# Graph-attention network on one core: the load phase's constants, centring, conversions and clearing in another order

## The chip, the cores and the metric

The kernel runs on one core of one Trainium2 chip. The metric is device time in microseconds (us) of that core. A core has five engines that work beside each other and meet by semaphores: TensorE (PE, matrix products, its weight loads shown as PEld), VectorE (DVE), ScalarE (ACT), GpSimd (POOL) and SyncE (SP), which here only issues transfers. Each engine runs its own list of instructions in the order written. Every engine's wait (`wait_ge`) holds back all that is queued behind it on that engine.

## The reference

Four graph layers run over one graph of 2048 nodes with 64 features. The adjacency matrix is a 2048 x 2048 int32 array. Every layer is preceded by a layer norm and a ReLU, and its result is added to x:

```
h = relu(layernorm(x)); x = x + gat(h, adj, W0, a0)
h = relu(layernorm(x)); x = x + gat(h, adj, W1, a1)
h = relu(layernorm(x)); x = x + two_step_gat_with_mlp(h, adj, ...)
h = relu(layernorm(x)); x = x + key_query_attention_with_powers(h, adj, ...)

gat(h, adj, W, a): Wh = h @ W
  e = leaky_relu((Wh @ a_src)[:, None] + (Wh @ a_dst)[None, :])
  att = softmax(where(adj > 0, e, -9e15), axis=1)
  return elu(att @ Wh)
```

The kernel counts four such attention passes (two of them inside the third layer) and the last one with keys and queries.

## The kernel before

**Tiling.** Nodes are split in 16 blocks of 128 (`NB`) and, the other way, in two column halves of 1024 (`NCH`). x lies transposed, 64 features times two strips on the 128 partitions, 512 columns for each column half. The adjacency comes as 32 blocks of 128 x 1024 int32 (512 KB each): blocks 0 to 15 are those of the first column half, 16 to 31 those of the second. They are staged in nine slots; a slot is loaded again when its block is converted. A block is converted twice: VectorE turns it into a bf16 mask in `nadj` (L1411), and an fp8 copy in `adj` is made by VectorE (L1418) for every third of the first 16 blocks, by ScalarE (L485) for the others.

**Constants.** One array `cst` of 128 x 1600 fp32 (800 KB) holds the identity (`ident`), the centring matrix (`center`), the columns that sum a strip (`half`), the weights `wt` with their transposes `wTt`, the attention vectors `av`, `lwT`, `atv`, `lbv`, and others. ScalarE issues its transfer (L406); SyncE issues x (L342) and then the blocks (L350). A second array `late` comes at the end of the list.

**Load phase, in the order of each engine.** TensorE waits for the constants, computes attention vectors of the third layer's passes (L611, L613) into the bank `M`, waits for VectorE to copy them (L1400, L1401), multiplies all attention vectors with the weights (L618), waits for VectorE to write these into the weight tile (L1404), and only then waits for x and centres it (`centre`, L631) into a PSUM bank of each column half. ScalarE squares the two centred halves (L411), VectorE clips them (L1138), TensorE sums the squares (`variances`, L651), VectorE writes the variances (L1143) and GpSimd takes their inverse roots (L372). TensorE then computes the norm of the weights (L861) and the features of both halves (`features`, L670), VectorE scales them by the roots (L1164, L1175), splits the row vector in three bf16 parts (L1185, L1130 to L1134), and TensorE and ScalarE spread it over the partitions (L678, L415, L685, L421). VectorE's list mixes `convert(n)` for the first nine blocks into this.

**First layer.** With the levels (L1201, L1204) TensorE takes a maximum over neighbours block by block (`chunk_levels`, L745), which needs the fp8 copies of blocks 0 to 15; the codes (L1258), products (L756), shifts (L427) and targets (L1270, L1274) follow. Then all four passes run over 16 blocks and two halves: VectorE writes the scores to PSUM (L1282), TensorE adds the mask (L763), ScalarE takes the exponential (L439), TensorE multiplies with the features (L771) and sums the rows (L791). In the first pass VectorE's list holds the conversions of the last blocks between the scores. The order of all lists is written out by hand.

**Clearing.** GpSimd clears small constants and `Kst` (L365) before the semaphore `consts` that all engines wait for; VectorE clears `Qst` (L1407) in the load phase. Both tiles are first written by `keys_split`, in the last layer.

Of the kernel before, what the change touches and what calls it, by code (L numbers as in the profile page):

```python
# [6 lines left out]
P = 128  # L7
N = 2048
F = 64
NB = N // P  # L10
CH = 1024
NCH = N // CH
# [4 lines left out]
GAT = 4  # L17
# [17 lines left out]
_at = 0  # L35
for _name, _width in (("ident", P), ("center", P), ("pick", 2), ("wt", GAT * 2 * (F + 2)),
                      ("half", 2), ("win", WIN), ("wTt", GAT * P), ("av", GAT * 2), ("lwT", 2 * P), ("atv", 2),
                      ("lbv", 2)):
    CONST[_name] = (_at, _width)
    _at += _width  # L40
WIDTH = _at
LATE = {"mw": (0, 3 * P), "wkq": (3 * P, 4 * EMB), "mb": (3 * P + 4 * EMB, 1),
        "restore": (3 * P + 4 * EMB + 1, P)}
# [3 lines left out]
def program(nc, xT_d, cst_d, late_d, adjT_d, out_d):  # L47
# [4 lines left out]
    with ctx:  # L52
# [6 lines left out]
        def sem(name):  # L59
            return ctx.enter_context(nc.semaphore(name))  # L60
# [110 lines left out]
        ld_x = sem("ld_x")  # L171
        ld_c = sem("ld_c")
        ld_late = sem("ld_late")
        ld_adj = [sem(f"ld_adj{k}") for k in range(SLOTS)]
# [100 lines left out]
        block = ctx.enter_context(nc.Block())  # L275
        N_C = 7

# [53 lines left out]
        def feat(hh):  # L331
            return slice(F * hh, F * (hh + 1))
# [7 lines left out]
        @block.sync  # L340
        def _(sp):
            sp.dma_start(x[:], xT_d.rearrange("c p n -> p c n")).then_inc(ld_x, 16)  # L342
            for n in range(NCH * NB):
                held = [m for m in range(n) if SLOT_OF[m] == SLOT_OF[n]]
                if held:
                    sp.wait_ge(adj_ready, held[-1] + 1)
                    if by_dve(held[-1]):
                        sp.wait_ge(adj8_dve, copies_by_dve(held[-1]))
                b = n % NB
                sp.dma_start(slot(n), adjT_d[b * P:(b + 1) * P, cols(n // NB)]).then_inc(ld_adj[SLOT_OF[n]], 16)  # L350
            sp.dma_start(late[:], late_d).then_inc(ld_late, 16)
            for c in range(NCH):
                sp.wait_ge(out_ready, c + 1)
                sp.dma_start(out_d[c], x[:, c, :]).then_inc(st_out, 16)
            sp.wait_ge(st_out, 16 * NCH)

        @block.gpsimd
        def _(pool):
# [5 lines left out]
            pool.memset(lnS[:], math.log(1 - SLOPE)).then_inc(consts, 1)  # L364
            pool.memset(Kst[:], 0.0).then_inc(consts, 1)  # L365
            pool.wait_ge(consts, N_C)
            n_root = [0]

# [36 lines left out]
        def _(act):  # L405
            act.dma_start(cst[:], cst_d).then_inc(ld_c, 16)  # L406
            act.wait_ge(consts, N_C)

            def square(n):
# [196 lines left out]
        def _(pe):  # L606
            pe.wait_ge(consts, N_C)
            pe.wait_ge(ld_c, 16)
            for l in range(2):
                for t in range(2):  # L610
                    pe.matmul(M[0:F, 2 * l + t:2 * l + t + 1], lwT[:, l, t * F:(t + 1) * F],  # L611
                              atv[:, l:l + 1], start=True, stop=True)
                last = pe.matmul(M[:, 8 + l:9 + l], lbv[:, l:l + 1].broadcast_to([32, P]), atv[:, l:l + 1],  # L613
                                 start=True, stop=True)
            last.then_inc(pe_prep, 1)
            pe.wait_ge(prep_ready, 1)
            for l in range(GAT):
                last = pe.matmul(M[:, 16 + 2 * l:18 + 2 * l], wTt[:, l, :], av[:, l, :], start=True, stop=True)  # L618
            last.then_inc(pe_prep, 1)
            pe.wait_ge(prep_ready, 3)  # L620
            pe.wait_ge(dve_const, 2)

            def repeat(bank_of, count):
# [223 lines left out]
            def key_rows(c):  # L847
# [4 lines left out]
                last.then_inc(kT_psum, 1)  # L852

            for n in range(NCH):
                if n == 0:
                    pe.wait_ge(ld_x, 16)
                centre(n)
            for n in range(NCH):
                variances(n)
            pe.wait_ge(wsq_ready, 1)  # L860
# [253 lines left out]
        def _(dve):  # L1114
# [254 lines left out]
            def keys_split(c):  # L1369

                link(dve.tensor_copy(parts[:, :, :, 0, :], kq[:]))
                link(dve.tensor_tensor(kqr[:], kq[:], parts[:, :, :, 0, :], ALU.subtract))
# [26 lines left out]
            dve.wait_ge(pe_prep, 1)  # L1399
            dve.tensor_copy(cb[:], M[:, 8:10])  # L1400
            dve.tensor_copy(av[:, 2:4, :], M[0:F, 0:4].rearrange("p (l t) -> p l t", l=2)).then_inc(prep_ready, 1)  # L1401
            dve.wait_ge(pe_prep, 2)
            for hh in range(2):
                dve.tensor_copy(wt4[feat(hh), :, hh, F:F + 2],  # L1404
                                M[feat(hh), 16:16 + 2 * GAT].rearrange("p (l t) -> p l t", l=GAT)).then_inc(prep_ready, 1)
            weight_squares()
            dve.memset(Qst[:], 0.0).then_inc(dve_const, 1)  # L1407

# [11 lines left out]

            convert(0)
            convert(1)
            for n in range(NCH):
                clip(n)
            for n in range(NCH):
                variance(n)
            convert(2)
            convert(3)
            weight_norms()
# [273 lines left out]
```

## Time and profile before

| what | value |
|---|---|
| three runs | 599.19, 594.17, 599.13 us; median 599.13 us |
| profiled execution's own time | 598.86 us |
| its span, first to last instruction | 597.1 us |
| mean granted TensorE clock | 0.974 |
| PE busy | 527.5 us, 88% |
| DVE busy | 393.9 us, 66% |
| ACT busy | 290.1 us, 49% |
| POOL busy | 30.8 us, 5% |
| HBM read | 18.40 MB |

Busy time is a share of the whole span. Matrix products are pipelined and their ends modelled, so a busy TensorE isn't one at its peak. The span is less than the execution's time by what lies around it. The granted clock is the share of 2.4 GHz that the chip lets TensorE have.

### The profile page before, as it was taken

Reading aid. Unit: us, or ns where it says so; the run is one execution under the profiler, and the core shown is the slowest. Engines: PE = TensorE matmul, PEld = TensorE weight load, DVE = VectorE, ACT = ScalarE, POOL = GpSimd, SP = SyncE. Lnnn points to the kernel's source line nnn. Section 1 sums busy time; section 2 is a strip of 40 time slices with the busy share of each in tenths; the row PEclk is TensorE's granted clock in tenths of the full one; section 3 lists DMA queues with packets and bytes.
Section 4 is the critical chain, followed back from the end, with each engine's and each line's share of the span. In section 5 each row is a group of like instructions: output and inputs, shape, how many; then the busy total and the mean of one; then the engine's idle time right before and its main releaser. Section 6 shows DMA issues by size and latency. Waiting matters only on the chain.

```text
span 597.1 us, 7591 instructions
## 1 busy us (share of the span) xinstructions
PE 527.5 (88%) x3136; PEld 198.5 (33%) x3136; DVE 393.9 (66%) x545; ACT 290.1 (49%) x314; POOL 30.8 (5%) x29
## 2 busy tenths in 40 slices
PE   4578997998998998998988998999868789999997
PEld 3422223343223343323243223344332234433332
DVE  2888779548989448989637989544999985110000
ACT  0487964524665525665524665446858685000000
POOL 1500000211000110000100000023000000000000
PEclk9788999999999999999989999999999899999999
DMA  8968100000000000000000000000000000000000
GB/s 323 343 235 290 45 1 0 1 2 1 0 1 1 2 0 2 1 1 0 1 1 1 1 2 1 0 1 2 0 0 1 0 2 0 1 2 0 1 8 28
DMA packets 5490, 19.40 MB, mean 32 GB/s; under 512 B 592, under 2 KB 592, under 8 KB 5456
## 3 DMA queue, kind: packets, MB, share of 16 engines
q1 hardware_dynamic: 5312, 18.11, 8.3%
q10 hardware_dynamic: 144, 0.82, 0.3%
q8 instruction: 24, 0.39, 0.3%
q14 instruction: 10, 0.08, 0.0%
HBM read 18.40 MB, written 0.52 MB: 32 GB/s over the span
## 4 chain that ended last, share of the span: by engine, by line
PE 57%; DVE 26%; ACT 7%; issue 7%; DMA 1%; POOL 1%; POOLq 0%; DVEq 0%; ACTq 0%
PE PROD L771 11%; PE X L1001 9%; DVE X L1282 9%; PE X L763 7%; PE PROD L1001 7%; PE S L791 6%; DVE aB L1550 6%; ACT big L439 4%; DVE big L1294 2%; DVE nadj L1567 2%; ACT big L485 1%; PE M L626 1%; DMA cst<-in_cst 1%; PE M L725 1%; DVE big L1291 1%
## 5 line engine op out<-in xcount | busy, mean ns | idle before, releaser
L439 ACT ACTIVATE big<-X,v 128x1024 f32<-128x1024 f32 x128 | 141.6, 1113 | 103.8 <-PE X L763 103.1
L1282 DVE SCALAR_TENSOR_TENSOR X<-wB,v,aB 128x1024 f32<-128x1024 f32 x128 | 163.4, 1294 | 27.7 <-ACT big L439 26.3
L771 PE MATMUL PROD<-big,Wh 128*64 128x512 f32 x512 | 135.7, 611 | 1.5 <-ACT big L439 1.3
L763 PE MATMUL X<-nadj,bigI 128*64 128x512 bf16 x512 | 77.9, 384 | 22.4 <-DVE X L1282 22.0
L763 PEld LDWEIGHTS X<-nadj,bigI 128*64 128x64 bf16 x512 | 25.5, 109 | 105.6 <-DVE X L1282 73.5
L791 PE MATMUL S<-big,onesf 128*32 128x512 f32 x400 | 53.3, 604 | 2.4 <-DVE big L1294 2.4
L771 PEld LDWEIGHTS PROD<-big,Wh 128*64 128x64 f32 x512 | 31.4, 136 | 51.9 <-issue 29.1
L1001 PE MATMUL PROD<-big,Wh 128*64 128x512 f32 x128 | 32.8, 634 | 9.7 <-ACT big L554 9.7
L372 POOL TENSOR_TENSOR rr<-var,mhalf 128x8 f32<-128x8 f32 x8 | 15.0, 1877 | 305.2 <-DVE var L1143 305.2
L1001 PE MATMUL PROD<-nadj,Wh 128*64 128x512 f32 x128 | 29.1, 598 | 0.4 <-ACT nadj L554 0.4
L1001 PE MATMUL X<-big,Wh 128*64 128x512 f32 x128 | 28.6, 595 | 0.0
L1001 PE MATMUL X<-nadj,Wh 128*64 128x512 f32 x128 | 28.0, 593 | 0.0
L485 ACT ACTIVATE big<-nadj 128x1024 fp8e4<-128x1024 bf16 x26 | 25.8, 1054 | 1.4 <-DVE nadj L1411 1.4
L1294 DVE TENSOR_TENSOR big<-big 128x1024 f32<-128x1024 f32 x21 | 25.6, 1219 | 0.4
L427 ACT ACTIVATE aB<-X,nvb,nvs 128x512 f32<-128x512 f32 x14 | 9.8, 775 | 25.5 <-PE X L756 25.5
L974 PE MATMUL X<-nadj,bigI 128*128 128x512 bf16 x64 | 19.3, 382 | 2.5 <-ACT big L544 1.4
L554 ACT ACTIVATE big<-big 128x1024 f32<-128x1024 f32 x16 | 16.8, 1057 | 8.8 <-DVE big L1567 8.8
L1567 DVE TENSOR_TENSOR nadj<-nadj,aB 128x1024 f32<-128x1024 f32 x16 | 18.4, 1218 | 3.0 <-ACT aB L550 2.9
L1567 DVE TENSOR_TENSOR big<-big,aB 128x1024 f32<-128x1024 f32 x16 | 19.4, 1224 | 0.5
L1411 DVE TENSOR_SCALAR nadj<-big 128x1024 bf16<-128x1024 int32 x28 | 18.9, 692 | 0.5 <-DMA big<-in_adjT 0.5
L977 PE MATMUL X<-wB 96*128 96x512 bf16 x64 | 19.1, 379 | 0.0
L1550 DVE TENSOR_TENSOR aB<-aB,big 128x1024 f32<-128x1024 f32 x15 | 18.4, 1224 | 0.4
(293 smaller groups left out, 574.7 us busy)
## 6 DMA issues: line engine op xcount, KB each, us to landing
big<-in_adjT SPq DMA_DIRECT2D x28, 512.0 KB, 6.9
aB<-in_adjT SPq DMA_DIRECT2D x4, 512.0 KB, 7.8
cst<-in_cst ACTq DMA_DIRECT2D x1, 800.0 KB, 5.8
x<-in_xT SPq DMA_DIRECT2D x1, 512.0 KB, 6.1
out<-x SPq DMA_DIRECT2D x2, 256.0 KB, 2.0
late<-in_late SPq DMA_DIRECT2D x1, 272.5 KB, 5.5
```

The lines of the kernel that those rows point to most:

```text
L439: act.activation(prob[:, t % U, :], X[t % 2][:], ACT.Exp, bias=v2[l % 2][:, k:k + 1]).then_inc(p_ready, 1)
L485: act.activation(adj[:, b, part], nadj[:, b, part], ACT.Identity, bias=1.0, saturate=False).then_inc(adj8_act, 1)
L763: last = pe.matmul(X[t % 2][feat(side), hh * BANK:(hh + 1) * BANK], bigI[:, feat(side)], nadj[:, k, half_cols(c, hh)], start=False, stop=T ...
L771: last = pe.matmul(PROD[c][feat(hh), :], Wh[l % 2][:, k, :], prob[:, t % U, hh * BANK:(hh + 1) * BANK], start=k == 0, stop=k == NB - 1)
L791: last = pe.matmul(S[32 * strip:32 * strip + 32, :], onesf[:, 0:32], src[:, hh * BANK:(hh + 1) * BANK], start=k == first_sum(c_all), stop= ...
L974: pe.matmul(X[s % 2][:, hh * BANK:(hh + 1) * BANK], bigI[:], nadj[:, jb, half_cols(c, hh)], start=True, stop=False)
L977: last = pe.matmul(X[s % 2][:, hh * BANK:(hh + 1) * BANK], KQ[0:KPAD, jb // CB, 1, (jb % CB) * P:(jb % CB + 1) * P], KQ[0:KPAD, c, 0, hh * ...
L1001: last = pe.matmul(out[feat(hh), :], src[:, jb, :], kept(c, jb)[:, hh * BANK:(hh + 1) * BANK], start=jb == 0, stop=jb == NB - 1)
L1282: dve.scalar_tensor_tensor(X[t % 2][:], wB[:, cols(c)], v8[l % 2][:, k:k + 1], aB[:, cols(c)], ALU.max, ALU.add).then_inc(x_written, 1)
L1294: ins = dve.tensor_tensor(acc[c], acc[c], prob[:, t % U, :], ALU.add)
L1550: ins = dve.tensor_tensor(accf[:, cols(c)], accf[:, cols(c)], kept(c, k), ALU.max)
L1567: dve.tensor_tensor(kept(c, k), kept(c, k), accf[:, cols(c)], ALU.add).then_inc(s_lowered, 1)
```

## The change

The constants are put in another order, so that `ident`, `center`, `half`, `lwT`, `atv`, `lbv` and `av` are its first 526 columns. SyncE loads these 526 columns first, then x, then block 0, then the other 1074 columns (`pick`, `wt`, `win`, `wTt`) with a semaphore of their own (`ld_w`), then the blocks from 1 on. TensorE centres x behind the first small products, and L618 moves between the variances of the two halves. The small products go to a corner of the bank `X[0]` instead of `M`. VectorE's list takes the first conversions apart. ScalarE gets one dummy activation ahead of everything. GpSimd clears both `Kst` and `Qst`, behind the semaphore `consts`, and `keys_split` waits for that.

```
-for _name, _width in (("ident", P), ("center", P), ("pick", 2), ("wt", GAT * 2 * (F + 2)),
-                      ("half", 2), ("win", WIN), ("wTt", GAT * P), ("av", GAT * 2), ("lwT", 2 * P), ("atv", 2),
-                      ("lbv", 2)):
+for _name, _width in (("ident", P), ("center", P), ("half", 2), ("lwT", 2 * P), ("atv", 2), ("lbv", 2),
+                      ("av", GAT * 2), ("pick", 2), ("wt", GAT * 2 * (F + 2)), ("win", WIN), ("wTt", GAT * P)):
+FIRST = CONST["pick"][0]
...
-        N_C = 7
+        N_C = 6
...
         def _(sp):
+            sp.dma_start(cst[:, 0:FIRST], cst_d[:, 0:FIRST]).then_inc(ld_c, 16)
             sp.dma_start(x[:], xT_d.rearrange("c p n -> p c n")).then_inc(ld_x, 16)
             for n in range(NCH * NB):
+                if n == 1:
+                    sp.dma_start(cst[:, FIRST:WIDTH], cst_d[:, FIRST:WIDTH]).then_inc(ld_w, 16)
...
-            pool.memset(Kst[:], 0.0).then_inc(consts, 1)
             pool.wait_ge(consts, N_C)
+            pool.memset(Kst[:], 0.0).then_inc(keys_clear, 1)
+            pool.memset(Qst[:], 0.0).then_inc(keys_clear, 1)
...
         def _(act):
-            act.dma_start(cst[:], cst_d).then_inc(ld_c, 16)
             act.wait_ge(consts, N_C)
+            act.activation(seed[:, 0:1], lnS[:], ACT.Square)
...
             pe.wait_ge(ld_c, 16)
             (the first small products: M becomes X[0])
             last.then_inc(pe_prep, 1)
-            pe.wait_ge(prep_ready, 1)
-            for l in range(GAT):
-                last = pe.matmul(M[:, 16 + 2 * l:18 + 2 * l], wTt[:, l, :], av[:, l, :], start=True, stop=True)
-            last.then_inc(pe_prep, 1)
-            pe.wait_ge(prep_ready, 3)
-            pe.wait_ge(dve_const, 2)
...
+            pe.wait_ge(ld_x, 16)
             for n in range(NCH):
-                if n == 0:
-                    pe.wait_ge(ld_x, 16)
                 centre(n)
-            for n in range(NCH):
-                variances(n)
+            variances(0)
+            pe.wait_ge(ld_w, 16)
+            pe.wait_ge(prep_ready, 1)
+            for l in range(GAT):
+                last = pe.matmul(X[0][:, 16 + 2 * l:18 + 2 * l], wTt[:, l, :], av[:, l, :], start=True, stop=True)
+            last.then_inc(pe_prep, 1)
+            variances(1)
+            pe.wait_ge(prep_ready, 3)
+            pe.wait_ge(dve_const, 2)
             pe.wait_ge(wsq_ready, 1)
...
             def keys_split(c):
+                dve.wait_ge(keys_clear, 2)
...
             dve.wait_ge(pe_prep, 1)
             (the copies to cb and av[:, 2:4]: M becomes X[0])
-            dve.wait_ge(pe_prep, 2)
-            for hh in range(2):
-                dve.tensor_copy(wt4[feat(hh), :, hh, F:F + 2],
-                                M[feat(hh), 16:16 + 2 * GAT].rearrange("p (l t) -> p l t", l=GAT)).then_inc(prep_ready, 1)
-            weight_squares()
-            dve.memset(Qst[:], 0.0).then_inc(dve_const, 1)
...
             convert(0)
+            clip(0)
             convert(1)
-            for n in range(NCH):
-                clip(n)
-            for n in range(NCH):
-                variance(n)
+            variance(0)
+            clip(1)
             convert(2)
+            dve.wait_ge(ld_w, 16)
+            dve.wait_ge(pe_prep, 2)
+            for hh in range(2):
+                dve.tensor_copy(wt4[feat(hh), :, hh, F:F + 2],
+                                X[0][feat(hh), 16:16 + 2 * GAT].rearrange("p (l t) -> p l t", l=GAT)).then_inc(prep_ready, 1)
+            weight_squares()
+            variance(1)
             convert(3)
             weight_norms()
```

## Rows read from the trace of the kernel before

**Rows 1.** The page: the span, and the transfer of the result to memory

```profile
span 597.1 us, 7591 instructions
...
out<-x SPq DMA_DIRECT2D x2, 256.0 KB, 2.0
```

**Rows 2.** The chain that ended last, from the start: start us, us, what

```profile
0.72 5.82 DMA cst<-in_cst
...
8.25 0.53 PE M L613 x2
9.07 1.88 PE M L618 x8
...
13.55 1.28 ACT L411
...
44.80 1.29 DVE X L1282
```

**Rows 3.** TensorE in order of time: start us, us, engine, line, tiles, shapes, count

```profile
11.39 3.48 PE L631 MATMUL PROD<-x,cst 128*128 128x512 f32 x4 [0.45 <-DVE cst L1404]
15.49 1.05 PE L651 MATMUL M<-cst,sq 128*128 128x2 f32 x8 [0.62 <-ACT sq L411]
16.41 1.03 PE L651 MATMUL S<-cst,sq 128*128 128x2 f32 x8
...
17.68 1.12 PE L670 MATMUL M<-cst,g 128*128 128x132 f32 x4
...
48.41 3.46 PE L771 MATMUL PROD<-big,Wh 128*64 128x512 f32 x8
...
54.64 1.94 PE L771 MATMUL PROD<-big,Wh 128*64 128x512 f32 x8
...
109.28 1.12 PE L635 MATMUL PROD<-x,cst 128*128 128x512 f32 x2
```

**Rows 4.** VectorE in order of time, 10 to 20 us

```profile
10.97 0.36 DVE L1404 COPY cst<-M 64x8 f32<-64x8 f32 x2 [1.96 <-PE M L618]
...
11.86 0.62 DVE L1411 TENSOR_SCALAR nadj<-big 128x1024 bf16<-128x1024 int32 x1
...
19.71 0.17 DVE L1164 TENSOR_TENSOR uv<-M,rr 128x8 f32<-128x8 f32 x1 [0.19 <-PE PROD L670]
```

**Rows 5.** Transfers issued in 0 to 12 us: count, KB, median us to landing

```profile
big<-in_adjT SPq DMA_DIRECT2D x8, 512.0 KB, 9.8
cst<-in_cst ACTq DMA_DIRECT2D x1, 800.0 KB, 5.8
x<-in_xT SPq DMA_DIRECT2D x1, 512.0 KB, 6.1
aB<-in_adjT SPq DMA_DIRECT2D x1, 512.0 KB, 13.2
```

**Rows 6.** Stretches: busy time by engine, granted clock, DMA share, GB/s

```profile
0.00:3.00 3.00, 0.00 (x0) 0.00 (x0) 0.00 (x0) 0.00 (x0) 1.50 (x11) 1.00 0.29 57
3.00:6.50 3.50, 0.00 (x0) 0.00 (x0) 0.00 (x0) 0.00 (x0) 0.00 (x0) 1.00 1.00 402
6.50:8.00 1.50, 1.33 (x9) 1.33 (x10) 0.36 (x2) 0.00 (x0) 0.00 (x0) 1.00 0.93 249
8.00:20.00 12.00, 10.61 (x46) 8.09 (x46) 6.68 (x19) 4.37 (x5) 2.76 (x2) 0.91 1.02 413
32.00:36.00 4.00, 3.89 (x22) 1.17 (x18) 4.00 (x8) 4.00 (x6) 0.00 (x0) 0.64 0.11 44
```

**Rows 7.** SyncE's issues in order of time: the first eight blocks

```profile
1.21 4.59 SPq L350 DMA_DIRECT2D big<-in_adjT  x8
```

**Rows 8.** GpSimd in order of time: the roots of the variances

```profile
17.24 3.71 POOL L372 TENSOR_TENSOR rr<-var,mhalf 128x8 f32<-128x8 f32 x2 [15.21 <-DVE var L1143]
```

**Rows 9.** Stretches, for TensorE's granted clock (the column before DMA share)

```profile
17.50:21.00 3.50, 3.50 (x17) 3.48 (x18) 3.24 (x10) 1.06 (x1) 3.50 (x3) 0.55 1.03 411
48.00:52.00 4.00, 4.00 (x14) 1.15 (x16) 4.00 (x5) 3.02 (x4) 0.00 (x0) 0.57 0.66 230
52.00:60.00 8.00, 8.00 (x58) 2.56 (x56) 6.18 (x9) 6.96 (x7) 0.00 (x0) 1.00 0.88 306
```

More of the change, by code:

```diff
@@ L172, in program @@
         ld_c = sem("ld_c")
+        ld_w = sem("ld_w")
+        keys_clear = sem("keys_clear")
         ld_late = sem("ld_late")
@@ L610, in _ @@
                 for t in range(2):
-                    pe.matmul(M[0:F, 2 * l + t:2 * l + t + 1], lwT[:, l, t * F:(t + 1) * F],
+                    pe.matmul(X[0][0:F, 2 * l + t:2 * l + t + 1], lwT[:, l, t * F:(t + 1) * F],
                               atv[:, l:l + 1], start=True, stop=True)
-                last = pe.matmul(M[:, 8 + l:9 + l], lbv[:, l:l + 1].broadcast_to([32, P]), atv[:, l:l + 1],
+                last = pe.matmul(X[0][:, 8 + l:9 + l], lbv[:, l:l + 1].broadcast_to([32, P]), atv[:, l:l + 1],
                                  start=True, stop=True)
             last.then_inc(pe_prep, 1)
-            pe.wait_ge(prep_ready, 1)
-            for l in range(GAT):
-                last = pe.matmul(M[:, 16 + 2 * l:18 + 2 * l], wTt[:, l, :], av[:, l, :], start=True, stop=True)
-            last.then_inc(pe_prep, 1)
-            pe.wait_ge(prep_ready, 3)
-            pe.wait_ge(dve_const, 2)
             def repeat(bank_of, count):
@@ L1399, in _ @@
             dve.wait_ge(pe_prep, 1)
-            dve.tensor_copy(cb[:], M[:, 8:10])
-            dve.tensor_copy(av[:, 2:4, :], M[0:F, 0:4].rearrange("p (l t) -> p l t", l=2)).then_inc(prep_ready, 1)
-            dve.wait_ge(pe_prep, 2)
-            for hh in range(2):
-                dve.tensor_copy(wt4[feat(hh), :, hh, F:F + 2],
-                                M[feat(hh), 16:16 + 2 * GAT].rearrange("p (l t) -> p l t", l=GAT)).then_inc(prep_ready, 1)
-            weight_squares()
-            dve.memset(Qst[:], 0.0).then_inc(dve_const, 1)
+            dve.tensor_copy(cb[:], X[0][:, 8:10])
+            dve.tensor_copy(av[:, 2:4, :], X[0][0:F, 0:4].rearrange("p (l t) -> p l t", l=2)).then_inc(prep_ready, 1)
             def mask_words(n):
```

## The prediction

> **What bounds the kernel now.** I first read the head of the page: the profiled execution spans 597.1 us [rows 1]. Its own time is 598.86 us, 1.76 us more for what lies around the span, and the median of the three runs is 599.13 us (594.17 to 599.19), so the profiled execution stands 0.27 us under the median. The page's shares over the whole span say nothing of a load phase of some 45 us, so the next view is the chain of waits from its start [rows 2]. In it the order is: the constants' transfer until 6.54 us, the first small products until 8.78 us, four more small products from 9.07 us, the centring of x, a 1.28 us table load on ScalarE, and from there a chain that reaches the first layer's first target (L1282) at 44.80 us. After that point layers follow each other by the same waits between engines; nothing in them is tied to absolute time. So what the change is worth is how much earlier the chain reaches 44.80 us, and whether it stays earlier.
>
> Third, the instructions in order of time, TensorE and VectorE [rows 3, 4]. TensorE centres x from 11.39 to 14.87 us and stands until 15.49 us for the squares; the features' product (L670) starts at 17.68 us and VectorE takes its result (L1164) at 19.71 us. From 19.71 us VectorE is busy nearly without a gap up to the levels, then ScalarE converts blocks back to back. Everything before 19.71 us is the stretch that the change rewrites, everything behind it is only moved. Fourth, the transfers: the constants and x, issued side by side on two queues, landed 5.8 and 6.1 us after issue [rows 5], and bytes flow at 402 GB/s from 3.0 us [rows 6].
>
> **The change, part by part.**
>
> *Constants in two parts, one queue.* The first part is 526 of 1600 columns, 263 KB; the second is 537 KB. On the load queue the order becomes first part, x, block 0, second part, block 1 and so on. By 3.0 us 3.0 x 57 = 0.17 MB have moved and then 402 GB/s [rows 6]; the first part (0.269 MB) is complete at 3.0 + 0.098/0.402 = 3.2 us, say 3.3 us at its semaphore. Bounds: a transfer of 256 KB lands in 2.0 us [rows 1], which gives 2.7 us; if landing doesn't depend on size, the constants' 5.8 us give 6.5 us. I take 3.3 us, near the row of its size. x is then complete at 3.0 + (0.793-0.171)/0.402 = 4.6 us, block 0 (1.317 MB) at 5.9 us. The rates of that view (402, then 249, then 413 GB/s) put the second part (1.867 MB) at 7.7 us and blocks 1, 2, 3 at 9.1, 10.4 and 11.6 us. SyncE issues two more transfers before block 1; at 0.57 us each (4.59 us for eight [rows 7]) all of the first eleven are issued by about 7 us, ahead of their bytes.
>
> The Trainium skill, "DMA: Bandwidth & Descriptors", section "Anatomy of one DMA", fits a software-issued transfer with 2.0 us plus its bytes over 436 GB/s. By it the first part lands at 0.72 + 2.0 + 0.62 = 3.3 us, an estimate from that page which agrees with mine; for the whole constants it gives 3.9 us, where this trace has 5.8 us, since here x was sharing the engines. The measurement decides.
>
> *The first products.* L611 and L613 follow the constants' landing by 8.78 - 6.54 = 2.2 us in all [rows 2], so they end at 5.5 us. Now TensorE goes straight to the centring (x has been there for 0.9 us) instead of waiting for VectorE's two copies and doing L618. Centring starts at 5.5 us where it started at 11.39 us: 5.9 us earlier. It takes 3.48 us [rows 3] and ends at 9.0 us.
>
> *The table load.* One dummy Square on ScalarE before any data takes the 1.28 us load [rows 2] out of the wait. ScalarE had its first input at 13.55 us, 2.16 us behind the start of centring; so now at 7.7 us, and a square takes (15.49-14.83) = 0.66 us: it is done at 8.3 us, before TensorE leaves the centring. The 0.62 us stand before the variances goes. If the load is not hoisted, the square ends at 9.6 us and 0.6 us of this come back.
>
> *What is put behind.* TensorE: variances(0) 9.0 to 9.9 us (16.41-15.49 = 0.92 us [rows 3]); then it waits for the second part (7.7 us, 2.2 us in hand; without that cover all behind it waits) and does L618, 1.86 us [rows 2], to 11.8 us; variances(1) and L861 take 17.68-16.41 = 1.27 us. The features start at 13.1 us, where they started at 17.68 us: 4.6 us earlier. L618 is only moved; the gain is its hidden wait, the constants' landing (3.2 us), the copies and the table.
>
> *VectorE's queue.* It now has convert(0) behind the two small copies (5.9 to 7.1 us, block 0 there at 5.9 us), clip(0) at 8.4 to 9.1 us, convert(1) to 9.7 us (block 1 at 9.1 us), variance(0) at about 10.1 us, clip(1) to 10.8 us, convert(2) to 11.5 us, the two copies of L1404 behind L618 (0.36 us [rows 4]) and the squares of weights to 12.4 us, variance(1) at 13.1 us or shortly before, convert(3), two passes of 0.6 to 0.7 us [rows 4], to 14.4 us, and the norms. The features' result arrives at 13.1 + 2.03 = 15.1 us. So the queue has 0.6 us in hand, and L1164 stands at 15.1 us against 19.71 us. Queued behind a late block here are variance(0), through it GpSimd's roots (3.71 us for two [rows 8]) and the features; the first root runs 10.1 to 12.0 us, the second to 14.9 us, both before they are asked for.
>
> *GpSimd's clearing.* Kst and Qst are cleared before 4 us on an idle engine; VectorE loses one memset of 0.38 us that stood in its wait. Zero, covered by GpSimd's wait for variance(0), and the new wait in keys_split lies hundreds of us later. The bank change from M to X[0] moves no instruction: zero.
>
> *Behind 15.1 us.* Conversions read blocks in the old order 4.6 us earlier. Do the transfers keep up? In 32 to 36 us the DMA engines were 11% busy [rows 6]: what held blocks back was slots freed by VectorE, not the engines, and slots are now freed 4.6 us earlier too. At 413 GB/s block 15 (9.7 MB) is there by 27 us and is asked for at about 31 us. Nothing is given back. Sum: 598.86 - 4.6 = **594.3 us**, 0.8% under the median shown.
>
> **The rivals.**
>
> *The constants' landing is mostly fixed.* With 5.8 us for the small part the centring starts at 8.8 us and the features at 16.4 us: 1.3 us gained, 597.5 us. For it: both transfers landed together near 6 us. Against: 1.58 MB had passed by then, which explains it by bytes.
>
> *TensorE's clock falls at better places.* It ran at its lower level (0.55 of 2.4 GHz granted) during the features, and again in 48 to 52 us at 0.57, behind a stretch in which it waited for the first targets [rows 9]. There eight L771 took 3.46 us against 1.94 us later [rows 3], 1.5 us; the centring's two pairs took 1.74 us each against 1.12 us for one pair at 109 us [rows 3], though the column prints 1.00 there. With the stretch at 48 us at 2.4 GHz and the 0.6 us of VectorE's slack used up by quick features: 594.3 - 1.5 - 0.6 = 592.2 us. For it: the shift moves the idle stretches against whatever the chip's observation is timed by. Against: the same idle stretches remain.
>
> The Trainium skill, "TensorE: Matmul & The Clock Gate", section on the HAM clock gate, says that the observation runs freely and doesn't start with the kernel, so one kernel shows different numbers of slow products in different runs. By that rule this case is a draw in each run, before and after; the spread of 594.17 to 599.19 us doesn't contradict it, no row here proves it.
>
> *The same clock, worse: the other side.* In the first layer TensorE, VectorE and ScalarE alternate pair by pair, and TensorE idles between. If blocks converted earlier leave its stretches thinner, the lower level holds for longer than one pair. Each further pair costs 1.5 us; from the fourth on the kernel is slower than before, with eight more it is at 594.3 + 12 = 606.3 us. Against it: the level is 1.00 from 52 to 60 us [rows 9] and those products stay the same.
>
> *Blocks late in front of variance(0).* The first eight blocks landed a median of 9.8 us after issue, the ninth 13.2 us [rows 5]. Block 1 is issued at about 2.9 us. VectorE needs 5.0 us from it to the features' result, so it must land after 14.7 us to be slower than before; at 13.2 us after issue it lands at 16.1 us and the time is 600.3 us. Against: those latencies are queueing behind bytes, and block 1 has only 2.4 MB up to its end.
>
> **How the numbers follow.** Forecast 0.54; landing mostly fixed 0.10; clock better 0.23; clock worse 0.07; blocks late 0.06. About 1% (6 us) is what a measurement of this kernel tells from no change. The forecast's own gain is 0.8%, so with the spread of the runs a quarter of it falls beyond 1%: 0.13. The better clock lies at 592.2 us, 1.15% under, four fifths beyond: 0.19. Faster 0.32. Slower by over 1% is the worse clock, 0.06. Same 0.62. Range: down to the better clock with the 2.7 us landing (592.2 - 0.6 = 591.6) and 0.6 us of run spread, 591.0 us; up to the fixed landing, 597.5 us, and 0.9 us of run spread, 598.4 us.
>
> **What would show it.** Right: the table load before 4 us; centring starts near 5.5 us; features near 13.1 us; L1164 near 15.1 us; the first L1282 near 40.2 us against 44.80 us; the rest shifted by the same. Wrong: VectorE waiting for a block between 9 and 13 us; TensorE waiting for the second part at 9.9 us; a wait for a block in front of the conversions of 28 to 36 us; a first L1282 that is early while the end is not, with eight L771 at 3.46 us more than once.

## The result, and the profile after

The changed kernel takes 595.35 us in the median of 20 runs (591.84 to 597.39) where the kernel before takes 597.33 us in 20 runs beside them (594.17 to 600.26). The medians lie 2.0 us apart (a quotient of 0.9967). The ratio measured over these runs, which isn't the quotient of the medians, is 0.9949, with a 95% interval of 0.9930 to 0.9968: 3.0 us faster, between 1.9 and 4.2 us. Ratios below are of this kind. The forecast was 4.6 us, and no change by the bound of 1%. In the changed kernel's profile the span is 590.5 us, 6.6 us less than before [rows 1]. More than half of that isn't the change's, as a second profile of the kernel before shows below.

Line numbers moved a little: L669 is the features' product (before L670), L860 the weights' product (L618), L650 the variances (L651), L630 the centring (L631), L1169 what takes the features (L1164), L1430 the copies of the weights (L1404), L1287 the first targets (L1282), L762 the masks of the passes (L763), L770 the products of the passes (L771).

The chain of waits of the changed kernel, from the start (start us, us, what):

```profile
2.61 8.34 DMA big<-in_adjT
...
11.07 0.70 DVE nadj L1411
...
13.08 0.15 DVE cst L1430
...
14.33 1.18 PE M L669 x4
...
30.27 5.68 ACT big L491 x6
...
42.32 1.29 DVE X L1287
```

Against [rows 2] the start of the chain is another one: no longer the constants, but the transfer of an adjacency block, until 10.95 us. The first target comes at 42.32 us instead of 44.80 us.

TensorE in order of time:

```profile
5.61 3.70 PE L630 MATMUL PROD<-x,cst 128*128 128x512 f32 x4
...
9.14 0.95 PE L650 MATMUL M<-cst,sq 128*128 128x2 f32 x8
...
10.02 1.05 PE L860 MATMUL X<-cst 64*128 64x2 f32 x8
...
11.00 1.05 PE L650 MATMUL S<-cst,sq 128*128 128x2 f32 x8
...
14.26 1.25 PE L669 MATMUL M<-cst,g 128*128 128x132 f32 x4
...
21.02 1.01 PE L677 MATMUL PROD<-identb,w 128*3 128x128 bf16 x8 [2.88 <-DVE w L1139]
...
46.32 3.62 PE L770 MATMUL PROD<-big,Wh 128*64 128x512 f32 x8
...
52.71 1.94 PE L770 MATMUL PROD<-big,Wh 128*64 128x512 f32 x8
```

Against [rows 3]: the centring starts 5.8 us earlier, and the first L650 and L860 stand where the forecast had them, within 0.2 us. The second L650 is 0.8 us ahead of it (11.0 against 11.8 us), since L860 took 1.05 us and not the 1.86 us of L618. Then TensorE waits for the weight tile, and the features start at 14.26 us, 1.2 us later than forecast.

VectorE in order of time:

```profile
8.41 0.69 DVE L1411 TENSOR_SCALAR nadj<-big 128x1024 bf16<-128x1024 int32 x1 [2.47 <-DMA big<-in_adjT]
9.02 0.69 DVE L1418 TENSOR_SCALAR big<-big 128x1024 fp8e4<-128x1024 int32 x1
9.62 0.69 DVE L1143 TENSOR_SCALAR g<-PROD 128x512 f32<-128x512 f32 x1
11.07 0.70 DVE L1411 TENSOR_SCALAR nadj<-big 128x1024 bf16<-128x1024 int32 x1 [0.77 <-DMA big<-in_adjT]
11.68 0.16 DVE L1148 TENSOR_SCALAR var<-M 128x8 f32<-128x8 f32 x1
...
13.08 0.35 DVE L1430 COPY cst<-X 64x8 f32<-64x8 f32 x2
...
16.42 0.17 DVE L1169 TENSOR_TENSOR uv<-M,rr 128x8 f32<-128x8 f32 x1 [1.32 <-PE PROD L669]
...
17.49 1.69 DVE L1411 TENSOR_SCALAR nadj<-big 128x1024 bf16<-128x1024 int32 x2
19.11 0.56 DVE L1190 TENSOR_SCALAR wS<-uv 128x8 f32<-128x8 f32 x1
```

Here is what failed: VectorE waits 2.47 us for block 0, until 8.41 us, and again for block 1 until 11.07 us. Variance(0), whose sums were there at 10.1 us, is written at 11.68 us, and the copies L1430, whose products were there at 11.1 us, are made at 13.08 us, behind the conversions of blocks 1 and 2 and a clip. L1169 stands at 16.42 us against 19.71 us [rows 4]: 3.3 us, not 4.6 us.

Transfers issued in 0 to 12 us (KB each, us to landing), and the rate in stretches (the last column is GB/s, the third from the end the granted clock):

```profile
big<-in_adjT SPq DMA_DIRECT2D x10, 512.0 KB, 10.6
cst<-in_cst SPq DMA_DIRECT2D x1, 537.0 KB, 7.6
x<-in_xT SPq DMA_DIRECT2D x1, 512.0 KB, 3.9
aB<-in_adjT SPq DMA_DIRECT2D x1, 512.0 KB, 12.9
cst<-in_cst SPq DMA_DIRECT2D x1, 263.0 KB, 2.7
```

```profile
3.00:5.00 2.00, 1.42 (x10) 1.42 (x10) 0.36 (x2) 0.00 (x0) 0.00 (x0) 1.00 0.94 345
5.00:8.00 3.00, 3.00 (x7) 1.75 (x7) 0.22 (x2) 0.28 (x1) 0.00 (x0) 1.00 0.96 269
8.00:20.00 12.00, 8.43 (x44) 7.17 (x42) 9.23 (x23) 3.03 (x4) 7.74 (x5) 0.69 1.02 413
```

The first part of the constants landed 2.7 us after issue (5.8 us for the whole before [rows 5]) and x 3.9 us after issue, at 5.0 us. But in 5 to 8 us only 269 GB/s flow, where I had counted on 402 GB/s until 6.5 us [rows 6]: the stretch in which block 0 is transferred. The Trainium skill, "DMA: Bandwidth & Descriptors", section "Anatomy of one DMA", fits a software-issued transfer with 2.0 us plus its bytes over 436 GB/s; an estimate from it for the first part, which SyncE issues here, is 2.0 + 0.62 = 2.6 us. The trace, with 2.7 us, agrees. What that page states about a single transfer doesn't give the slow block.

### The profile page after: what moved, and what is told of

It is laid out like the page before. It is cut to its first block, busy times and chain, and to the rows that moved or that the text cites. A ratio compares the mean times of both kernels' runs of the same rounds, so it can differ in the third digit from the quotient of the medians.

```text
span 590.5 us, 7592 instructions
## 1 busy us (share of the span) xinstructions
PE 525.4 (89%) x3136; PEld 196.6 (33%) x3136; DVE 393.7 (67%) x544; ACT 290.7 (49%) x315; POOL 31.7 (5%) x30
## 4 chain that ended last, share of the span: by engine, by line
PE 55%; DVE 27%; ACT 7%; issue 7%; DMA 1%; POOL 1%; POOLq 0%; SPq 0%; DVEq 0%; ACTq 0%
PE PROD L770 11%; PE X L1006 9%; DVE X L1287 9%; PE X L762 7%; PE PROD L1006 6%; PE S L790 6%; DVE aB L1556 6%; ACT big L445 4%; DVE big L1299 2%; DVE nadj L1573 2%; DMA big<-in_adjT 1%; ACT big L491 1%; PE M L625 1%; PE M L724 1%; DVE big L1296 1%
## 5 line engine op out<-in xcount | busy, mean ns | idle before, releaser
L1287 DVE SCALAR_TENSOR_TENSOR X<-wB,v,aB 128x1024 f32<-128x1024 f32 x128 | 163.4, 1293 | 28.3 <-ACT big L445 26.9
L770 PE MATMUL PROD<-big,Wh 128*64 128x512 f32 x512 | 135.9, 612 | 1.5 <-ACT big L445 1.3
L762 PE MATMUL X<-nadj,bigI 128*64 128x512 bf16 x512 | 78.8, 388 | 22.0 <-DVE X L1287 21.6
L762 PEld LDWEIGHTS X<-nadj,bigI 128*64 128x64 bf16 x512 | 25.6, 110 | 105.6 <-DVE X L1287 72.5
L770 PEld LDWEIGHTS PROD<-big,Wh 128*64 128x64 f32 x512 | 31.6, 137 | 52.3 <-issue 29.1
```

What stands on the lines that cost most here:

```text
L762: last = pe.matmul(X[t % 2][feat(side), hh * BANK:(hh + 1) * BANK], bigI[:, feat(side)], nadj[:, k, half_cols(c, hh)], start=False, stop=T ...
L770: last = pe.matmul(PROD[c][feat(hh), :], Wh[l % 2][:, k, :], prob[:, t % U, hh * BANK:(hh + 1) * BANK], start=k == 0, stop=k == NB - 1)
L1287: dve.scalar_tensor_tensor(X[t % 2][:], wB[:, cols(c)], v8[l % 2][:, k:k + 1], aB[:, cols(c)], ALU.max, ALU.add).then_inc(x_written, 1)
```

## The experiments

Times of a profile are of one execution, ratios are to the kernel before on the same chip with their 95% interval. "The lower clock" is read from what the same products take: the variances take 0.95 to 1.05 us or 1.71 to 1.87 us (once 1.24 us), L860 takes 1.05 or 1.86 us.

**1. Conversions behind what they hold up.** The changed kernel with VectorE's list in another order:

```
+            clip(0)
             convert(0)
-            clip(0)
-            convert(1)
             variance(0)
             clip(1)
-            convert(2)
             dve.wait_ge(ld_w, 16)
             ... (copies of the weights, weight_squares)
+            convert(1)
             variance(1)
+            convert(2)
             convert(3)
```

> The changed kernel with VectorE's first conversions put behind what they hold up (clip, convert 0, variance 0, clip, copies of the weights, convert 1, variance 1, convert 2, 3). Theory A (blocks 0 and 1 land at 8.4 and 11.1 us, later than I forecast, and hold the variances and the copies in VectorE's queue): the copies L1430 move from 13.1 to about 11.1 us, the features start at 12.4 instead of 14.3 us, L1164/L1169 stands at 15.1 instead of 16.4 us and the first target at about 41.0 us instead of 42.3 us; time 1.2 us under the changed kernel, ratio to before 0.993. Rival B (the missing gain is TensorE's clock and ScalarE's list): L1169 earlier but the first target stays at 42.3 us and the ratio at 0.995.

Ratio 0.9904 (0.9881 to 0.9926). VectorE in order of time:

```profile
8.34 0.69 DVE L1143 TENSOR_SCALAR g<-PROD 128x512 f32<-128x512 f32 x1 [2.41 <-ACT sq L417]
...
11.52 0.36 DVE L1428 COPY cst<-X 64x8 f32<-64x8 f32 x2 [0.31 <-PE X L860]
...
13.79 0.69 DVE L1411 TENSOR_SCALAR nadj<-big 128x1024 bf16<-128x1024 int32 x1 [0.30 <-DMA big<-in_adjT]
...
15.07 0.16 DVE L1169 TENSOR_TENSOR uv<-M,rr 128x8 f32<-128x8 f32 x1
...
41.09 1.29 DVE L1287 SCALAR_TENSOR_TENSOR X<-wB,v,aB 128x1024 f32<-128x1024 f32 x1
```

The copies come at 11.52, L1169 at 15.07 and the first target at 41.09 us: theory A to within 0.4 us, and rival B, by which the first target stays, falls. L1169 is where my forecast had it (15.1 us): the order of VectorE's list was the missing 1.3 us. The ratio lies outside the changed kernel's interval, and it is lower than theory A's 0.993: 5.7 us under the kernel before, where the first target is 3.7 us earlier. What makes up the other 2 us isn't shown.

**2. Constants whole, on ScalarE's queue.** The changed kernel with the split of the constants and their move to SyncE's queue undone:

```
-            sp.dma_start(cst[:, 0:FIRST], cst_d[:, 0:FIRST]).then_inc(ld_c, 16)
-                if n == 1:
-                    sp.dma_start(cst[:, FIRST:WIDTH], cst_d[:, FIRST:WIDTH]).then_inc(ld_w, 16)
+            act.dma_start(cst[:], cst_d).then_inc(ld_c, 16)
(waits for ld_w become waits for ld_c)
```

> The changed kernel with the constants whole on ScalarE's queue again, beside x. Theory A (the early landing of the first part is most of the gain): the first products start at 6.6 us instead of 3.6 us, centring at 8.8 us instead of 5.6 us, L1169 at 17.6 us or later, the first target at 43.5 us, ratio to before 0.997. Rival B (VectorE is bound by its blocks, so the early constants are hidden behind them): L1169 stays within 0.4 us of 16.4 us and the ratio is 0.995.

Ratio 0.9981 (0.9956 to 1.0005). Centring started at 8.03 us instead of 5.61 us, but the features at 14.87 instead of 14.26 us and L1167, which takes them, at 17.03 us: 0.6 us behind the changed kernel, between the two theories; the first target came at 42.95 us, 0.6 us behind too. By these marks 2.4 us of early centring are worth 0.6 us as long as VectorE stands for blocks. The ratio lies above both that were expected (0.997 and 0.995): its interval holds theory A's 0.997, just leaves out rival B's 0.995, and reaches 1.0005, so that this kernel isn't shown to be faster than the one before.

**3. The table load alone**, ahead in the kernel before.

```
             act.wait_ge(consts, N_C)
+            act.activation(seed[:, 0:1], lnS[:], ACT.Square)
```

> The kernel before with nothing but the dummy activation that pulls the table load ahead. Theory A (the load was on the chain only for what the centring of the second half did not cover): the variances start at 14.9 instead of 15.5 us, L1164 at 19.1 instead of 19.7 us, 0.6 us, ratio 0.999. Rival B (the whole 1.28 us was on the path): 18.4 us and ratio 0.998.

Ratio 1.0001 (0.9977 to 1.0025), and in the profile L1165, which takes the features, is not earlier but at 21.06 us. TensorE in order of time:

```profile
15.03 1.71 PE L652 MATMUL M<-cst,sq 128*128 128x2 f32 x8
...
16.60 1.84 PE L652 MATMUL S<-cst,sq 128*128 128x2 f32 x8
```

The variances started at 15.03 instead of 15.49 us, but took 1.71 and 1.84 us where [rows 3] has 1.05 and 1.03 us: they ran at TensorE's lower clock in this execution. 0.5 us was gained, and 1.5 us and more was lost by the clock: neither theory is decided.

**4. The weights' products ahead of the centring.** The changed kernel with L618's products, behind the wait for the second part, put back ahead of `centre`.

```
+            pe.wait_ge(ld_w, 16)
+            pe.wait_ge(prep_ready, 1)
+            (the products of wTt and av)
             pe.wait_ge(ld_x, 16)
             for n in range(NCH):
                 centre(n)
             variances(0)
-            (wait for ld_w and prep_ready, the products of wTt and av)
             variances(1)
```

> The changed kernel with L618's products (here behind the wait for the second part) ahead of the centring again, as before the change. Theory A (the second part lands at 9.7 us and all of TensorE's work queues behind it): centring starts at 11.5 us, L1169 stands at about 19.5 us, the first target at about 44.8 us, no gain over before (ratio 1.000). Rival B (the order on TensorE is worth little since VectorE is held by its blocks): L1169 at about 17.5 us, ratio 0.997.

Ratio 1.0005 (0.9983 to 1.0027): the whole gain is gone, as theory A has it. TensorE in order of time:

```profile
10.05 1.86 PE L856 MATMUL X<-cst 64*128 64x2 f32 x8 [4.39 <-DMA cst<-in_cst]
11.84 3.78 PE L630 MATMUL PROD<-x,cst 128*128 128x512 f32 x4
15.42 1.71 PE L650 MATMUL M<-cst,sq 128*128 128x2 f32 x8
```

TensorE stands 4.39 us for the second part. L1169 came at 21.91 us instead of 19.5 us and the first target at 47.40 us instead of 44.8 us: this execution too had its variances at the lower clock. Splitting the constants gains only together with centring ahead of the weights.

**5. GpSimd's copies x - 1 later**, on top of experiment 1.

```
+            pool.wait_ge(p_ready, 6)
             for c in range(NCH):
                 below_one(c)
```

> The first experiment's kernel (conversions behind what they hold up), and GpSimd's two copies x - 1 (below_one), which ran beside VectorE's split from 16.2 to 19.8 us, held until six exponentials of the first layer are done. Theory A (GpSimd's tensor work slows VectorE beside it: two L1411 took 1.70 instead of 1.30 us, L1190 0.57 instead of 0.16, L1135 0.55 instead of 0.18): these come back to 1.30, 0.16 and 0.18 us, features of the second half at 18.7 instead of 19.9 us, first target at about 40.0 instead of 41.1 us, ratio to before 0.988. Rival B (ScalarE's list sets the first target, whatever VectorE does): VectorE faster, first target unchanged at 41.1 us, ratio 0.990.

Ratio 0.9891 (0.9858 to 0.9925), median 591.59 us: the fastest kernel of all, though its interval holds experiment 1's 0.9904. VectorE in order of time:

```profile
17.09 0.17 DVE L1170 TENSOR_TENSOR uv<-M,rr 128x8 f32<-128x8 f32 x1 [0.52 <-PE PROD L670]
...
18.16 1.28 DVE L1412 TENSOR_SCALAR nadj<-big 128x1024 bf16<-128x1024 int32 x2
19.36 0.17 DVE L1191 TENSOR_SCALAR wS<-uv 128x8 f32<-128x8 f32 x1
...
20.60 0.17 DVE L1170 TENSOR_TENSOR uv<-S,rr 128x8 f32<-128x8 f32 x1
...
56.11 1.10 DVE L1412 TENSOR_SCALAR nadj<-aB 128x1024 bf16<-128x1024 int32 x1
```

From the features of the first half to those of the second it took 3.5 us, in experiment 1 (15.07 to 19.85 us) 4.8 us, in the changed kernel (16.42 to 21.00 us) 4.6 us, and 1.28 and 0.17 us stand where the changed kernel has 1.69 and 0.56 us. And where GpSimd's copies now run, from 55.96 us, one L1412 takes 1.10 us instead of 0.69 us. So theory A holds for VectorE: GpSimd's pass over x delays VectorE's short instructions. The Trainium skill, "SBUF — State Buffer", section "Who interferes with whom", says that copies, casts and tensor_scalar instructions can take a mode that locks a port pair shared with GpSimd for a whole instruction; the trace agrees for these, which stretch in the changed kernel, but they aren't the only ones: in the kernel before, the 0.17 us of a tensor_tensor, L1131 at 22.42 us beside the same copies, became 0.54 us. The first target was at 41.52 us and not at 40.0 us, because the variances and the weights' products again ran at the lower clock (L861 took 1.87 us) and the features started at 14.92 instead of 12.61 us.

**6. A small reading of the adjacency ahead.**

```
+            act.dma_start(touch[:], adjT_d[0:P, 0:64]).then_inc(ld_touch, 16)
```

> The changed kernel with one more small transfer, 128 rows of 256 bytes of the adjacency, issued by ScalarE at the start into a tile that nothing reads. It asks why block 0 took 3.6 us of packets (4.4 to 8.0 us) where later blocks take 1.3 us. Theory A (the first reading of the adjacency array is slow on each DMA engine, whichever block it is): the small transfer takes that, block 0 lands at about 7.1 instead of 8.4 us and block 1 at about 10 instead of 11.1 us. Rival B (block 0 competes with something else in 5 to 8 us, or the start of the stream is slow): landing at 8.4 us or later.

Ratio 0.9956 (0.9930 to 0.9982). Block 0 was there at 8.28 us, block 1 at 11.17 us (8.41 and 11.07 us without), and the rate in 5 to 8 us was 269 GB/s as before. A first reading of 32 KB doesn't make block 0 quick.

**7. Blocks 1 and 0 exchanged** in the load queue.

```
-            for n in range(NCH * NB):
-                if n == 1:
+            for n in [1, 0] + list(range(2, NCH * NB)):
+                if n == 0:
                     sp.dma_start(cst[:, FIRST:WIDTH], ...)
```

> The changed kernel with blocks 1 and 0 exchanged in the load queue. Theory A (whichever block comes first is slow): block 1 lands at about 8.4 us, block 0 at about 11.1 us; L1169 at about 18.3 us since the conversion of block 0 is first in VectorE's list. Rival B (block 0's own rows are slow to read): block 1 lands at about 7.1 us, block 0's packets stretch over 3 us.

One timed execution, 596.73 us. VectorE waited for block 0, now second, until 10.47 us, where block 1 in this place came at 11.07 us; 333 instead of 269 GB/s in 5 to 8 us. L1169 stands at 17.75 us, with the variances at the lower clock. Between the two theories: the block in front is slow whichever it is, but block 1 is less so.

**8. The changed kernel again.**

> The changed kernel once more. Theory A (the load phase is the same from run to run, what differs is where TensorE's clock falls): block 0 waits until 8.4, L1169 at 16.4, first target at 42.3 us, each within 0.5 us, while the stretches at the lower clock and the end of the span differ from the first profile by up to 3 us; ratio to before between 0.993 and 0.997. Rival B (the landing of block 0 is chance): it moves by more than 1 us.

Ratio 0.9948 (0.9923 to 0.9973). Block 0 at 8.81 us, block 1 at 11.49 us, L1169 at 16.84 us, within 0.5 us of the first profile. The first target came at 43.80 instead of 42.32 us and the span was 592.5 us. Theory A holds up to the features; behind them this execution lost another 1.1 us, and here TensorE's products ahead of the first target ran at the lower clock:

```profile
37.91 2.08 PE L755 MATMUL X<-gridz,c 32*128 32x512 f32 x4
```

They took 1.13 us in the first profile. So the first target too moves by 1.5 us between two executions of one kernel, three times what theory A allowed.

**9. Block 0 ahead of x** in the load queue.

```
-            sp.dma_start(x[:], ...)
             for n in range(NCH * NB):
                 if n == 1:
+                    sp.dma_start(x[:], ...)
                     sp.dma_start(cst[:, FIRST:WIDTH], ...)
```

> The changed kernel with block 0 ahead of x in the load queue (first part of the constants, block 0, x, second part, block 1). Theory A (the first block of the adjacency is slow wherever it stands): its packets again take 3 us or more, it lands at 6.5 us or later and drags x behind it, centring starts at 7 us or later. Rival B (what slows it lies in the stretch of 5 to 8 us): block 0 lands at about 4.9 us, x at about 6.0 us, centring starts at 6.2 instead of 5.6 us, and whatever is transferred in 5 to 8 us is slow instead. In either case L1169 is not earlier than 16.4 us by more than 0.5 us.

Ratio 0.9946 (0.9923 to 0.9970). Stretches of its trace, columns as above:

```profile
3.00:5.00 2.00, 1.46 (x10) 1.46 (x10) 0.36 (x2) 0.00 (x0) 0.00 (x0) 1.00 0.88 249
5.00:8.00 3.00, 0.87 (x5) 0.77 (x5) 1.51 (x4) 0.00 (x0) 0.00 (x0) 1.00 0.95 371
```

The slow stretch has moved with the block, from 5 to 8 us to 3 to 5 us, and x landed 6.1 us after issue and started the centring at 7.76 us. That is theory A in what matters; block 0 itself was converted from 6.04 us, a little ahead of the 6.5 us expected. The slowness belongs to the block at the front, not to the time. Though block 0 was there early and x late, the ratio is that of the changed kernel: what VectorE no longer waits for, TensorE does. The profile doesn't bear out that much: its variances ran at the lower clock, L1169 came at 19.25 us and the first target at 45.00 us, no earlier than in the kernel before.

**10. Dummy products in TensorE's waits**, on top of experiment 5.

```
+            for _ in range(4):
+                pe.matmul(X[1][:, 0:P], c16[:], c16[:], start=True, stop=True)
             pe.wait_ge(ld_c, 16)
...
+            pe.wait_ge(adj_ready, 1)
+            repeat(X[0], 6)
             for n in range(NCH):
                 w_rows(n)
                 w_broadcast(n)
+                if n == 0:
+                    repeat(X[0], 3)
...
+                if l == 0:
+                    pe.wait_ge(wB_ready, 4)
+                    repeat(PROD[0], 10)
                 mask(l, 0, 0)
+                if l == 0:
+                    repeat(PROD[0], 3)
                 mask(l, 0, 1)
```

> The kernel of the later x - 1 copies, with dummy products in TensorE's waits of the load phase: four of c16 while the constants are on their way, six and three of the mask's first columns while VectorE splits the rows, ten and three ahead of and between the first two masks. They write banks that nothing reads. It adds work and takes none away. Theory A (TensorE's lower clock costs the load phase 1.5 us at the centring or the variances and 1.5 us at the first L770 pairs): centring takes 2.3 instead of 3.8 us, eight L770 take 1.9 instead of 3.5 us, ratio to before 0.985. Rival B (the lower clock lies where others are waited for, or the dummy products don't lift it): within 0.1% of the kernel without them, 0.989.

Ratio 0.9909 (0.9889 to 0.9928). The four products ahead did nothing: centring took 3.78 us and L863, the weights' products, 1.87 us. The thirteen ahead of the masks did what they were for. TensorE, then VectorE, in order of time:

```profile
45.23 1.02 PE L773 MATMUL PROD<-big,Wh 128*64 128x512 f32 x4
46.61 1.08 PE L773 MATMUL PROD<-big,Wh 128*64 128x512 f32 x4 [0.35 <-ACT big L446]
...
48.97 0.62 PE L765 MATMUL X<-nadj,bigI 128*64 128x512 bf16 x4 [0.85 <-DVE X L1299]
...
51.39 1.94 PE L773 MATMUL PROD<-big,Wh 128*64 128x512 f32 x8
```

```profile
54.94 1.29 DVE L1299 SCALAR_TENSOR_TENSOR X<-wB,v,aB 128x1024 f32<-128x1024 f32 x1 [1.77 <-ACT big L446]
```

The first eight products took 2.1 us instead of 3.46 us [rows 3]. Yet the fourth pair's target stands at 54.94 us, where the kernel without them has 54.91 us: in between TensorE waited 0.85 us for a score of VectorE, which has conversions of blocks between its scores. Rival B is right for the time: the ratio is a little above its 0.989, which the interval just holds. The lower clock of the first L773 costs nothing here, since VectorE's conversions take as long.

**11. The kernel before again.**

> The kernel before once more, for its profile. Theory A (the load phase repeats, the later layers differ by where the clock falls): L1164 at 19.7 and the first target at 44.8 us within 0.5 us if TensorE's clock falls at the same places; up to 1.7 us later if the variances run at the lower clock; the end differs by up to 3 us. Rival B (the 6.6 us between the first two spans are the change's): the span is 597 us again within 0.5 us.

L1164 at 19.49 us and the first target at 44.56 us, within 0.3 us, but a span of 592.0 us instead of 597.1 us. The same stretch of both traces of the kernel before, the first profile and then this one:

```profile
300.00:316.00 16.00, 14.01 (x114) 6.67 (x118) 7.60 (x25) 3.90 (x6) 0.00 (x0) 0.79 0.01 2
468.00:482.00 14.00, 10.62 (x44) 4.95 (x40) 10.94 (x12) 6.30 (x8) 0.00 (x0) 0.76 0.00 0
```

```profile
300.00:316.00 16.00, 13.45 (x140) 6.37 (x134) 9.03 (x31) 3.90 (x6) 0.00 (x0) 1.00 0.01 2
468.00:482.00 14.00, 10.91 (x58) 4.30 (x56) 13.03 (x14) 9.88 (x12) 0.00 (x0) 1.00 0.00 1
```

The first profile was granted 0.79 and 0.76 of the clock there, the second 1.00. That is the 5 us between two executions of one kernel, and rival B falls: against this trace the changed kernel's span is 1.5 us shorter, not 6.6 us.

**12. The changed kernel without the dummy activation.**

```
-            act.activation(seed[:, 0:1], lnS[:], ACT.Square)
```

> The changed kernel without the dummy activation, so that the table load stands before the first square again. Theory A (in the changed kernel the load is hidden, since VectorE waits for blocks 0 and 1 until 11.1 us anyway): the first square at 9.0 instead of 7.7 us, the first variances 0.5 us later, but L1169 at 16.4 us plus or minus 0.4 as in the two profiles of the changed kernel (16.42 and 16.84). Rival B (my forecast's 0.6 us for it holds): L1169 at 17.0 to 17.5 us with TensorE's clock as there.

One timed execution, 596.74 us. The square started at 9.01 us, the clip of the first half at 9.73 us (9.62 us with it) since VectorE had the conversion of block 0 in front of it anyway. L1168, which takes the features, came at 17.74 us, but with the lower clock: the first variances, the weights' products and the second variances took 1.87 us each. Experiment 6's kernel, with the same waits for blocks, the same lower clock and the dummy activation, had it at 17.32 us. That is 0.4 us for the load where the clock is low, or 0.7 us if each is counted from its own start of the centring (5.56 and 5.84 us). Neither theory had this time. At the higher clock this run doesn't show it.

## Why the prediction was right, and where it wasn't

Its range and its sign held; its size was 4.6 us against 3.0 us (1.9 to 4.2). That the forecast of 594.3 us lies only 1.1 us under the measured 595.35 us is luck in part: the sum started from the profiled execution's 598.86 us, 1.5 us above the median of the kernel's 20 runs, and this hides part of the gain that was forecast too large. The terms, by the prediction's own steps:

*Constants in two parts, the first products, what is put behind:* right for TensorE. The first part landed at 3.4 us (forecast 3.3), centring started at 5.61 us (5.5), the variances at 9.14 us (9.0), L860 at 10.02 us (9.9), without a wait for the second part. That cover was thin: the second part was forecast for 7.7 us and landed at 9.7 us, and in the second profile TensorE waited 0.15 us for it. Experiment 4 shows the price of losing that order: all of it.

*VectorE's queue:* wrong. "Block 0 there at 5.9 us" and "block 1 at 9.1 us" were worked out from the rate at which x and the constants had moved. The block at the front moves slower: they were there at 8.4 and 11.1 us. The "0.6 us in hand" turned into a wait of 2.47 us and one of 0.77 us, and L1169 came at 16.42 us instead of 15.1 us. It is the rival "blocks late in front of variance(0)" with a smaller size: block 1 at 11.1 us, short of the 14.7 us from which I put it slower than before. Experiment 1 shows it: with the same late blocks, but nothing urgent behind them, L1169 stands at 15.07 us. That this is the forecast's own number is luck in part: the features started 0.5 us ahead of the forecast (12.61 against 13.1 us), and VectorE, still converting, took their result 2.46 us after they started, where it took 2.03 us in the kernel before. The sign of the lateness was in the trace before: 249 GB/s in 6.5 to 8 us [rows 6], which I used as a rate of that time instead of asking which transfer was under way.

*"Nothing is given back":* wrong by 0.8 us between L1169 and the first target (3.3 us down to 2.5 us). No block was late there, as forecast. The kernel before, VectorE and TensorE:

```profile
23.89 0.17 DVE L1164 TENSOR_TENSOR uv<-S,rr 128x8 f32<-128x8 f32 x1
```

```profile
23.91 0.61 PE L678 MATMUL PROD<-identb,w 128*3 128x128 bf16 x8 [2.50 <-DVE w L1134]
```

0.4 us went to VectorE's instructions beside GpSimd's copies of x, which had met other instructions before: the features of the second half came at 21.00 us against 23.89 us, 2.9 us earlier. Another 0.4 us went to L677 at the lower clock, 1.01 us where the kernel before had 0.61 us, and that is a matter of the execution: in the second profile it took 0.61 us. Experiment 5 shows the first; the second is read from traces only. Behind the first target another 0.6 us went: the second group of eight L770 starts at 52.71 us against 54.64 us [rows 3], 1.9 us earlier. The masks before it (L762) took 1.07 and 1.06 us where the kernel before has 0.62 us twice, and the first group of L770 took 3.62 against 3.46 us: again the lower clock.

*The 0.6 us of the table load:* not shown as such. Experiment 3 lost it under the clock, experiment 12 makes it 0.4 to 0.7 us with the clock low.

*GpSimd's clearing and the banks at zero:* no run undoes them alone; both memsets of GpSimd ended at 2.83 us, before anything waited.

*The clock rivals:* neither came true in the profile. Eight L770 took 3.62 us after the change and 3.46 us before, once in each. From one execution of a kernel to the next the clock does more than that (experiments 8 and 11). The Trainium skill, "TensorE: Matmul & The Clock Gate", section on the HAM clock gate, says that the observation runs freely and doesn't start with the kernel; the two profiles of the kernel before, 5 us apart with the same instructions, don't contradict it, and no run here proves it. *The landing mostly fixed:* fell, 2.7 us.

*Marks and ratios* don't add up. At the second group of L770 the changed kernel is 1.9 us ahead in its first profile and 1.1 us in its second (53.55 us), and the ratio says 3.0 us. Experiment 1 is 3.8 us ahead (50.84 us), and its ratio says 5.7 us. Experiment 9 has no lead at the first target, and its ratio is that of the changed kernel. Each mark is of one execution, and behind the load phase two executions of one kernel differ by 5 us by the clock. Whether the shift also changes how often the later layers fall to the lower clock, no run tests. So the experiments show what the order of the lists does to the load phase; that this is all of the 3.0 us isn't shown.

What also stays open: why the block at the front of the adjacency is slow. It follows the block (experiment 9) and not the time, is somewhat less with block 1 in front (experiment 7), and a small reading ahead doesn't help (experiment 6).

## What to carry to other kernels

When an engine's list mixes work on arriving data with work on the critical chain, put the chain's instructions first wherever the arrival isn't certain: two late blocks in front cost 1.3 us of a 4.6 us gain at the features, and moving the urgent lines ahead of them gave that back. Read a transfer rate from the rows of the same tensor, not from whatever ran at that time. And compare a short phase by its own marks (here the first target) in more than one profile of each kernel, since spans of one kernel differ by 5 us; look at the durations of the products ahead of the mark too, since the mark itself moved by 1.5 us with the clock.

## What the runs showed of the hardware

While the adjacency's first block in the queue was under way, the rate was 245 to 333 GB/s in 5 to 8 us in the nine profiles with the split constants ahead of x and x ahead of the block, 249 GB/s in 3 to 5 us with the block ahead of x, and 229 to 249 GB/s in 6.5 to 8 us in the four with the constants whole. In 8 to 20 us it is 412 to 415 GB/s.

TensorE's centring ran at the lower level for all or most of its time in every execution (3.4 to 3.8 us for two pairs against 1.12 us for one at 109 us [rows 3]) while the clock column prints 1.00: in the load phase the duration of a product says more than the column. Where the centring took 3.40 to 3.70 us (five profiles), the variances behind it took 0.95 to 1.05 us; where it took 3.78 us (nine profiles), they took 1.24 to 1.87 us.

Beside GpSimd's pass over 128 x 512 values a VectorE instruction of 0.17 us lasted 0.56 us, and one of 0.69 us lasted 1.10 us.
